# A transpose on TensorE moved from ahead of a tile's gate and up products to behind their first six

## The reference

```python
y = x @ W_base.T + scaling[a] * (((x @ Wt.T) @ A[a].T) @ B_w[a].T) @ Wp.T   # a: the adapter of the batch row
probs = softmax(y @ gate_w.T)                 # 16 experts
top2, idx = top_k(probs, 2); top2 /= top2.sum()
g = y @ w_gate[e].T ; u = y @ w_up[e].T        # 512 -> 352, for the token's two experts
h = silu(g) * u
out = x + sum_e top2[e] * (h @ w_down[e].T)    # 352 -> 512
```

## Time and profile before

| | |
|---|---|
| time, median of 3 runs | 343.33 us |
| the runs | 343.33, 341.28, 343.49 us |
| the profiled execution | 341.91 us |
| its span, first to last instruction | 340.1 us |
| PE busy | 329.9 us, 97% |
| DVE busy | 235.5 us, 69% |
| ACT busy | 180.0 us, 53% |
| POOL busy | 128.9 us, 38% |
| mean granted TensorE clock | 0.995 of full |

### The profile page before, as it was taken

One profiled execution on the slowest core, in us unless ns is written; L12 is line 12 of the kernel. 1 busy time (PEld: TensorE's weight loads), 2 busy tenths in 40 slices (PEclk: granted clock), 3 DMA queues, 4 the chain that ended last, 5 costly groups with the idle time before them and its releaser, 6 DMA issues.

```text
span 340.1 us, 7756 instructions
## 1 busy us (share of the span) xinstructions
PE 329.9 (97%) x1847; PEld 290.7 (85%) x1847; DVE 235.5 (69%) x314; ACT 180.0 (53%) x246; POOL 128.9 (38%) x85
## 2 busy tenths in 40 slices
PE   7999999989999999999999999999999999999992
PEld 5657788879999999989988999989999989989981
DVE  3639799896646677584886948788586588779310
ACT  4368823623466444556646365485555476574321
POOL 0000000112634635556382653745645281534313
PEclk9999999999999999999999999999999999999997
DMA  7975887749599899999999997999979979931153
GB/s 270 411 290 238 308 331 254 268 154 324 169 347 290 182 271 263 296 216 271 246 263 288 324 345 183 286 307 300 314 179 268 248 210 275 308 42 26 17 74 44
DMA packets 47927, 82.47 MB, mean 243 GB/s; under 512 B 5552, under 2 KB 22576, under 8 KB 47792
## 3 DMA queue, kind: packets, MB, share of 16 engines
q1 hardware_dynamic: 38912, 62.96, 56.1%
q0 software_dynamic: 8960, 18.89, 25.4%
HBM read 60.59 MB, written 19.92 MB: 237 GB/s over the span
## 4 chain that ended last, share of the span: by engine, by line
PE 95%; DMA 1%; issue 1%; ACT 1%; POOLq 1%; DVE 0%; ACTq 0%
PE bank L707 46%; PE bank L736 24%; PE bank L681 4%; PE bank L455 4%; PE bank L492 3%; PE bank L571 3%; PE bank L572 3%; PE bank L573 3%; DMA lead_sb<-lead 1%; PE bank L581 1%; PE bank L609 1%; PE bank L624 1%; POOLq L96 0%; PE bank L529 0%; DVE hh L1201 0%
## 5 line engine op out<-in xcount | busy, mean ns | idle before, releaser
L1288 POOL DMA_INDIRECT out<-ys,sidx x40 | 79.9, 1997 | 115.8 <-DMA out<-ys,sidx 65.9
L362 DVE TENSOR_TENSOR w_lo<-w_raw,w_hi (+2 forms) x32 | 76.2, 2380 | 11.2 <-issue 9.3
L1267 POOL DMA_INDIRECT xg<-y_rows,gidx x40 | 48.5, 1212 | 91.7 <-issue 75.4
L707 PE MATMUL bank<-w_hi,xt_hi 128*128 x320 | 82.0, 333 | 1.1 <-ACT y_st L802 1.1
L707 PE MATMUL bank<-w_hi,xt_lo 128*128 x320 | 79.0, 323 | 0.0
L707 PE MATMUL bank<-w_lo,xt_hi 128*128 x320 | 78.9, 323 | 0.0
L360 ACT ACTIVATE w_hi<-w_raw (+2 forms) x32 | 64.7, 2021 | 9.5 <-DMA w_raw<-wall 5.6
L871 ACT ACTIVATE sg<-bank 128x352 f32<-128x352 f32 x40 | 18.5, 463 | 77.1 <-PE bank L707 70.0
L707 PEld LDWEIGHTS bank<-w_hi,xt_hi 128*128 128x128 f32 x320 | 54.7, 189 | 2.5 <-issue 1.7
L707 PEld LDWEIGHTS bank<-w_hi,xt_lo 128*128 128x128 f32 x320 | 56.1, 189 | 0.0
L707 PEld LDWEIGHTS bank<-w_lo,xt_hi 128*128 128x128 f32 x320 | 56.1, 188 | 0.0
(11 more groups left out here) (188 smaller groups left out, 363.3 us busy)
## 6 DMA issues: line engine op xcount, KB each, us to landing
w_raw<-wall SPq DMA_DIRECT2D x16, 1408.0 KB
w_raw<-wall SPq DMA_DIRECT2D x16, 768.0 KB
xs<-xg SPq DMA_DIRECT2D x132, 64.0 KB
y_rows<-y_st SPq DMA_DIRECT2D x16, 256.0 KB, 6.8
x_st<-xin SPq DMA_DIRECT2D x6, 512.0 KB, 13.5
lead_sb<-lead SPq DMA_DIRECT2D x4, 512.0 KB, 5.4
head_sb<-head SPq DMA_DIRECT2D x2, 640.0 KB, 8.8
wb_sb<-wb SPq DMA_DIRECT2D x2, 512.0 KB, 11.5
```

Source lines behind the costliest of these rows:

```text
L362: e.tensor_tensor(w_lo[:, bass.ds(dst, n)], raw, hi, ALU.subtract).then_inc(own, 1)
L707: mm = e.matmul(bank[2 + 2 * s + t % 2][:, 0:INTER], a, w[:, bass.ds(at + (k * GU + s * INTER), INTER)], start=k == 0 and i == 0, stop=k = ...
L1267: e.indirect_dma_start(out=xg[t % NXG][:], out_offset=None, in_=y_dram, in_offset=bass.IndirectOffsetOnAxis(ap=gidx[:, t:t + 1], axis=0)). ...
L1288: e.indirect_dma_start(out=out, out_offset=bass.IndirectOffsetOnAxis(ap=sidx[:, t:t + 1], axis=0), in_=ys[t % NYS][:], in_offset=None, bou ...
```

## The change

`h_turn(t-1)` for t = 3 to 32 no longer stands at the head of the loop's step, ahead of `x_turn(t+1)` and `gate_up(t)`. It is called inside `gate_up(t)`, at k = 1, so behind the six matmuls of k = 0. For t = 2 it stays at k = 2. The turns of tiles 32 to 39 stay where they are, and nothing is changed on the other engines.

```diff
@@ gate_up(t)
                     for k in range(KH):
                         if t == 0 and k == KH // 2:
                             x_turn(e, count, 1)
-                        if t == 2 and k == KH // 2:
+                        if 2 <= t <= NFULL and k == (KH // 2 if t == 2 else 1):
                             h_turn(t - 1)
@@ the loop
                 for t in range(2, NTILE + 1):
                     go_on(e, rest, count, t - 1)
-                    if 3 <= t <= NFULL:
-                        h_turn(t - 1)
                     if t + 1 < N_PE:
                         x_turn(e, count, t + 1)
```

## The result

The changed kernel took 344.56 us in the median of 20 runs (342.86 to 346.99); the kernel before, run beside it, 343.41 us in the median of 20 (340.81 upward). The ratio is 1.0052, with a 95% interval of 1.0034 to 1.007: slower by half a per cent. (A ratio is worked out from the runs within 1.5% of their kernel's fastest, a median from all runs, so it isn't the quotient of the two medians.) Two more batches, of 12 runs of the changed kernel each, gave 1.002 (0.9987 to 1.0053) and 1.0019 (0.9988 to 1.005), which alone can't be told from no change. The forecast was 343.9 us and no change that counts; the measured time lies 0.7 us above it and inside the range of 341.4 to 345.4. That range holds "no change" (343.3) as well, so the time by itself says little for the mechanism; the traces have to.

The account below looks back on a forecast made before the run. The prediction took PE's own work to bound the kernel. Its terms, -1.14 removed and +0.75, +0.49 and +0.47 lost, summed to +0.57 us on the median of 343.33: 343.9 us, range 341.4 to 345.4 us.

Parts of the forecast that it names:

- What bounds the kernel; the move's own cost: Tile loop: PE's own work sets the time, busy 97%; moving the turn costs 0.00 us of PE time.
- What it removes, -1.14 us: PE's waits ahead of moved turns, hidden by 0.97 us of matmuls: tile 16 -0.91, tile 30 -0.18, tile 4 -0.05.
- the term for tile 16: Turn of tile 16, late behind a weight load ACT awaited 2.07 us: the whole PE loss goes, -0.91 us.
- What it delays, 0.72 us: ACT and DVE behind the turn: h_evac and h_low come 0.72 us later, h_evac starting 1.50 after the old turn.
- The pattern of new experts, +0.75 us: Eight gate_ups from tile 8 to 28 wait for DVE's later weight split: 0.02 to 0.13 us each, +0.75 in all.
- Tiles 31 and 32: gate_up(31) waits for its late split, +0.49 us; the unmoved turn of tile 32 waits for its late product, +0.47.
- The sum: Whole kernel: -1.14 + 0.75 + 0.49 + 0.47 = +0.57 us, put on the median of 343.33 for 343.9.
- the lead at 0.05 us: Semaphore to PE's first weight load, taken as 0.20 us; at the lower bound 0.05, total -0.39 us, 342.9.
- Only the gain: Rival, tile loop: weights' low half comes early enough everywhere, so -1.14 us stays; 342.2 us, chance 0.20.
- Nothing to hide: Rival, moved turns: tile 16's late load is only that execution's, so nothing changes; 343.3 us, chance 0.10.
- More late loads are hidden: Rival, weight loads: longer runs hold two stalls like tile 16's, each giving back 0.9; -1.9, 341.4 us, chance 0.12.
- Slower, in every new expert: Rival, gate_up of new experts: all nine tiles lose 0.49 us waiting for weights; +3.7, 347.0 us, chance 0.07.

Follow-up runs that it names:

- e6: The kernel before with an idle ACT copy of 4 x 344 elements ahead of silu in tiles 7 to 31; 358.72 us, ratio 1.0477.
- e7: The changed kernel with an idle ACT copy of 4 x 344 elements ahead of silu in tiles 7 to 31; 345.13 us, ratio 1.009.
- e1: The changed kernel with the turn of tile 31 put back ahead of gate and up of tile 32, the other 29 moved; 343.11 us, ratio 0.999.
- a_again: The changed kernel run and traced once more, nothing altered; 344.42 us, ratio 1.002 to the kernel before.
- b_again: The kernel before run and traced once more, nothing altered; 343.24 us, ratio 1.0002.
- e9: The changed kernel run and traced for the third time, nothing altered; 343.31 us, ratio 1.0019 to the kernel before.
- e2: The changed kernel with the 30 turns behind the first two matmuls of gate_up in place of six; 343.38 us, ratio 0.9983.
- e4: The changed kernel with DVE's weight split ahead of h_low, and down taking h's low half last, from tile 7 on; 342.89 us, ratio 0.9998.
- before: The kernel before, without the move, in the execution profiled for the prediction; 343.41 us median beside the changed kernel, ratio 1.
- e5: The kernel before, turn in its place, with an idle ACT copy of 2 x 344 elements ahead of h_evac in tiles 7 to 31; 346.95 us, ratio 1.015.
- e3: The kernel before with DVE's weight split ahead of h_low, and down taking h's low half last, from tile 7 on; 342.81 us, ratio 1.0006.
- e8: The changed kernel with DVE's weight split ahead of h_low and down taking h's low half last, run a second time; 342.86 us, ratio 1.0008.

## Why the prediction was right, step by step

**What bounds the kernel; the move's own cost.** Right, with one row misread: the 2.5 us of the earlier trace rows, captioned as PE's idle time, are 0.53 us of idle matmuls and 1.97 of idle weight loads. The sum didn't use the row but went by the timeline, so nothing hangs on it. A turn inside gate_up costs PE the same 0.24 to 0.25 us and 0.08 behind it, and gate_up behind `down` starts without a loss (0.48 us for the first pair at 163.80).

**What it removes, -1.14 us.** The mechanism was right: e6 against e7 shows the room, and e1's tile 12 shows it in use. Mis-sized: the term for tile 16, -0.91, was read off one execution, and put on the median. Once more traced, the kernel before lost 0.43 there. This is the first term that failed in size, and it alone brings the forecast from +0.57 to +1.05 us; the medians gave +1.15 in the first batch and +0.70 and +0.29 in the two others. That no moved turn waits in the three traces of the changed kernel is no proof for this term, as the load of tile 16 wasn't late in them.

**What it delays, 0.72 us.** Right to 0.01: 1.50 us from gate_up's start to h_evac.

**The pattern of new experts, +0.75 us.** Nine periods of 6.36 to 6.39 us in a_again against 6.28 to 6.32 in b_again: 57.38 against 56.77 us in all, +0.61. The time from the split's end to the load, taken as 0.20 us, was 0.18. By its bounds of 0.05 and 0.50 this one number held from nothing to 2.7 us more, and it was the row of the register work that chose well. Tile by tile the terms were less good than their sum: gate_up(21), (23) and (25) lost 0.08, 0.05 and 0.06 where 0.13 each was forecast, gate_up(28) 0.06 in place of 0.02, and gate_up(18) 0.10 in place of nothing, as the load of tile 16 wasn't late. Three plain periods came out 0.04 to 0.05 us shorter than before.

The page "TensorE: Matmul & The Clock Gate" of the Trainium skill (section "Part 3: Packing small matmuls — row/col tiling") lets a load overlap matmuls only on other row groups. The loss here was 0.08 us behind a load of 0.19, so the trace disagrees in the changed kernel too.

**Tiles 31 and 32.** Period 29 grew from 6.44 to 6.72 us, +0.28, where -0.18 + 0.49 = +0.31 was forecast. Period 31 grew from 6.57 to 7.25, +0.68, where +0.47 was forecast: mis-sized. The turn came 0.47 us late, where 0.42 was forecast, but what stood behind it came later still. After `down(31)` the turn is followed by the step's two branches, of which the first runs at 291.2 and the second at 291.4, and by gate_up's waits, the last of which ran at 291.8; with no lead they come out on PE: gate_up started 0.70 us behind the turn in place of 0.41. I had put 0.05 on it, from tile 16, where there was no branch behind.

**The sum.** Of a_again against b_again: +0.61 + 0.28 + 0.68 - 0.43 = +1.14 us, less 0.24 in plain and early periods, which is the 0.9 us of tile part. The -0.43 is b_again's stall, which a_again had no late load for; that the move took it away isn't shown. Without it the difference is +1.33 us, and +1.46 for e9; against the trace I predicted from, without its 0.91, +1.78 and +1.91. The forecast's own terms without tile 16 make +0.57 + 0.91 = +1.48, so its cost side was good. The forecast was right in sign and too small by the two terms above. It stays a change of a fifth to a half per cent. Two smaller slips: with the lead at 0.05 us the terms add up to -0.34 (343.0 us), not -0.39; and a measurement told 0.5% from no change, where the prediction allowed itself 1%.

**The rivals.** *Only the gain* fell on tiles 29 and 31 and the nine periods; it would have come true with a delay of 0.07 in place of 0.72 us (e2), or with the split taken out of the way (e4). *Nothing to hide*: its condition held in the three traces of the changed kernel, in which the load of tile 16 wasn't late, but the change's own costs are there all the same. *More late loads are hidden*: such loads exist in both orders, but ACT's waits for them at tile 16 were 0.93 to 2.07 us or 3.64 to 5.25 us, the latter beyond the room, and two stalls of 0.91 make 1.8 us, not 1.9. The price also left out the change's own costs, which late loads don't take away. Between b_again and `before`, and between a_again and e9, the spans differ by 1.4 and 2.4 us, and the time ahead of the tiles by 1.6 and 2.4; other runs weren't traced. *Slower, in every new expert*: the mechanism is the real one, and e5 shows its size where nothing balances it (+4.4 us); here v_gu came 0.21 us ahead of the slot (169.89 to 170.10), where 0.22 was put.

## What to carry to other kernels

A step moved later on the bounding engine buys room for what it waits for and takes the same room from what waits for it. Follow it down the in-order queue of each engine that it feeds, with the operation that stands behind the fed one (here a 3 us weight split behind a 0.56 us subtraction), not only to the fed result. The room should be as large as the lateness seen and no larger: a turn behind two matmuls cost almost nothing here, behind six it cost more than it brought. The same holds for a queue that is put in another order: the split ahead of h_low took the loss away and brought a wait for h_low where something came late. And a stall seen in one execution is priced by a second trace, before it goes into a sum for the median.

## What the runs showed of the hardware

So a wait of 2.1 us cost 3.9: 8.57 and 7.95 us in place of two periods of 6.3. In e3 PE stood 3.72 us, the granted clock was 0.50 from 191.5 to 194.8 us, and the period was 5.6 us longer. The waits of PE of 1.71 us in e1 and of 1.99 us in e7 and in e8 left the granted clock at 1.00, and the periods with them were 1.9 to 2.2 us longer. So of four stalls of 1.7 to 2.1 us one cost nearly twice its length, the other three little more than their own.

The part ahead of the tiles, the same code in all kernels, ended at either 85.9 to 86.4 us or 87.7 to 88.3 us in 13 traces, with nothing between. What decides between the two wasn't tried.
